# A graph layer and a mixture of experts on one core: the last stage's seven groups processed in five units

## The reference, cut to what matters

```
x = x + gnn(layernorm(x))        # gnn: [gat(W0) , gat(W1)] + input, then layer norm, * gamma + beta
x = x + ffn(layernorm(x))        # ffn: 8 experts, each node goes to its best 2

gat:   alpha over the edges into a node (softmax per head, 8 heads x 16 channels)
       out = segment_sum(xw[src] * alpha)
ffn:   logits = x @ Wg + bg;  top 2 -> softmax of the two logits
       out += w * (gelu(x @ W1[e] + b1[e]) @ W2[e] + b2[e])   for the 2 chosen experts
```

## Time and profile before

| | us |
|---|---|
| median of 3 runs (3034.85 to 3039.28) | 3036.93 |
| the profiled execution | 3038.06 |
| its span | 3036.2 |
| VectorE busy | 2092.3 (69%) |
| TensorE busy | 2122.6 (70%) |
| GpSimd busy | 1891.8 (62%) |
| ScalarE busy | 1786.1 (59%) |

### The profile page before, as it was taken

One profiled execution on the slowest core, in us unless ns is written; L12 is line 12 of the kernel. 1 busy time (PEld: TensorE's weight loads), 2 busy tenths in 40 slices (PEclk: granted clock), 3 DMA queues, 4 the chain that ended last, 5 costly groups with the idle time before them and its releaser, 6 DMA issues.

```text
span 3036.2 us, 42924 instructions
## 1 busy us (share of the span) xinstructions
PE 2122.6 (70%) x11674; PEld 2009.3 (66%) x11675; DVE 2092.3 (69%) x4422; ACT 1786.1 (59%) x2613; POOL 1891.8 (62%) x1868
## 2 busy tenths in 40 slices
PE   4600003778887888888878888603449999999998
PEld 2400003778887788787878787603438999999997
DVE  7678867777777777777777777788864444444443
ACT  5424424888888888888888888624433333333332
POOL 5777777777777777777777777777771222222222
PEclk8855556889998999898999898855559999999999
DMA  9446994444444444444444444555772222222222
GB/s 356 135 145 180 159 239 122 127 127 158 132 127 127 143 147 127 128 158 131 128 127 158 133 127 128 170 206 174 260 258 37 37 38 37 38 38 37 38 37 31
DMA packets 278910, 395.04 MB, mean 130 GB/s; under 512 B 156236, under 2 KB 231569, under 8 KB 272257
## 3 DMA queue, kind: packets, MB, share of 16 engines
q1 hardware_dynamic: 202945, 244.92, 25.8%
q0 software_dynamic: 74000, 145.58, 21.6%
q10 hardware_dynamic: 1840, 3.06, 0.3%
HBM read 201.61 MB, written 191.79 MB: 130 GB/s over the span
## 4 chain that ended last, share of the span: by engine, by line
POOL 47%; PE 25%; issue 16%; DVE 5%; DMA 2%; DVEq 1%; ACT 1%; SPq 1%; POOLq 0%; ACTq 0%
POOL AR L932 43%; PE ps L1440 12%; PE ps L1446 12%; POOL adstart L894 1%; POOL placed L999 1%; DMA tables<-AR 1%; POOL room L971 1%; DVE group_stats L1987 1%; ACT AR L1258 1%; DVE AR L1705 1%; SPq L379 0%; SPq L609 0%; DVE AR L2111 0%; DVE AR L2108 0%; DVE AR L2047 0%
## 5 line engine op out<-in xcount | busy, mean ns | idle before, releaser
L932 POOL DMA_INDIRECT AR<-tables,idx x1391 | 1329.8, 956 | 425.8 <-issue 423.5
L1354 PE MATMUL ps<-table_parts,onehot 128*128 128x408 f32 (+1 forms) x5848 | 1194.2, 369 | 304.5 <-ACT onehot L1214 213.3
L1354 PEld LDWEIGHTS ps<-table_parts,onehot 128*128 128x128 f32 x5848 | 1160.0, 208 | 338.7 <-DVE AR L1817 185.3
L1139 ACT COPY AR<-AR 128x1984 f32<-128x1984 f32 (+3 forms) x110 | 402.6, 3660 | 255.4 <-DVE AR L1752 212.6
L1008 POOL DMA_INDIRECT out<-AR,idb x105 | 185.0, 1762 | 567.6 <-issue 536.6
L1752 DVE TENSOR_TENSOR_SCAN AR<-ps,AR 128x512 f32<-128x512 f32 x404 | 454.2, 1197 | 0.0
L1440 PEld LDWEIGHTS ps<-AR 128*128 128x128 f32 x3360 | 393.2, 193 | 31.8 <-issue 26.5
L1440 PE MATMUL ps<-AR 128*128 128x128 f32 x3360 | 393.8, 276 | 26.4 <-DVE AR L2205 26.4
L1745 DVE TENSOR_TENSOR AR<-AR,ps 128x3968 f32<-128x3968 f32 (+1 forms) x51 | 357.5, 7010 | 5.8 <-ACT AR L1158 5.8
L1214 ACT ACTIVATE onehot<-onehot 128x2048 fp32r<-128x2048 f32 (+1 forms) x172 | 347.6, 2021 | 5.5
L2205 DVE COPY AR<-AR 128x1024 f32 x210 | 151.6, 722 | 207.2 <-PE ps L1440 205.7
(11 more groups left out here) (342 smaller groups left out, 2345.5 us busy)
## 6 DMA issues: line engine op xcount, KB each, us to landing
state<-AR SPq DMA_DIRECT2D x50, 2232.0 KB, 9.5
AR<-tables,idx POOLq DMA_INDIRECT x1440
AR<-in_L_ffn_W SPq DMA_DIRECT2D x16, 1024.0 KB, 9.7
AR<-placed SPq DMA_DIRECT2D x420, 32.0 KB
AR<-adstart SPq DMA_DIRECT2D x50, 248.0 KB, 4.0
adstart<-room SPq DMA_DIRECT2D x21, 496.0 KB, 13.5
tables<-AR SPq DMA_DIRECT2D x49, 136.0 KB
room<-tables SPq DMA_DIRECT2D x14, 476.0 KB, 4.4
```

The costliest lines, as they stand in the source:

```text
L932: pool.indirect_dma_start(out=G[s][:, j, 0:ROWT], out_offset=None, in_=table_rows, in_offset=bass.IndirectOffsetOnAxis(ap=idx[:, s, j:j + ...
L1139: return S.copy(to.rearrange("p j (h c) -> p j h c", h=HD)[:, :, :, a:z], of[:, :, 1:n + 1].rearrange("p (c h) j -> p j h c", h=HD)[:, :, ...
L1354: return T.matmul(bank[:, 0:z], mark, table_parts[:, k, v * w:v * w + z], start=(a == 0 and k == 0), stop=(a == LEV - 1 and k == PARTS - 1))
```

## The change

Groups are taken in units. `UNITS` for conv1 and all that follows is (0), (1), (2, 3), (4, 5), (6); `UNITS2` for conv2 is (0, 1), (2, 3), (4), (5, 6). The small instructions of a unit of two work on 14 tiles at once: `shares`, the weights (now a function of its own, `weights`), the scales, `choose`, `settle` and their waits. The per-tile instructions stay one for each tile, and `combine` (the products and sums of whole rows) and `conclude` stay one for each group. `ranks` of a pair has 16 products rather than 9. The buffers of the small values hold 14 tiles, the shares no longer two groups in turn.

The order changes on every engine:

- VectorE, unit u: `weights`, `combine` of its groups, statistics with the next unit's shares meanwhile, `choose(u - 1)`, `conclude` of its first group, `settle(u - 1)`, `conclude` of the second, second statistics (with conv2's last shares at u = 1, and its last pair behind them).
- ScalarE: the exponential of the next unit's shares stands ahead of the normalisation, that of the gate behind the first group's normalisation.
- GpSimd: conv2's group 6 is gathered ahead of conv1's 2, and conv1's 4 and 5 are gathered ahead of the first placement; group 6 of conv1 follows the placement of unit 0. A unit's placements go in one run.
- SyncE: `OWN_ORDER` takes conv2's 5 and 6 ahead of conv1's 2, and loads and stores follow the units.

The core of the diff:

```diff
+UNITS = ((0,), (1,), (2, 3), (4, 5), (6,))
+UNITS2 = ((0, 1), (2, 3), (4,), (5, 6))
+OWN_ORDER = ((1, 0), (1, 1), (1, 2), (1, 3), (1, 4), (0, 0), (0, 1), (1, 5), (1, 6), (0, 2), (0, 3), (0, 4), (0, 5), (0, 6))
...
             last_states2(5, 2, GRP)
-            for n in range(2, 4):
+            last_states2(6)
+            for n in range(2, 6):
                 last_states1(n)
-            last_states2(6)
...
-            for n in range(NG):
-                place(n)
-                if n + 4 < NG:
-                    last_states1(n + 4)
+            for u, unit in enumerate(UNITS):
+                pool.wait_ge(places_ready, u + 1)
+                for i, n in enumerate(unit):
+                    for k in range(2):
+                        for t in range(GRP):
...
+                if u == 0:
+                    last_states1(6)
...
+            for u, unit in enumerate(UNITS):
+                deviations(u, 0)
+                if u + 1 < NU:
+                    share_exps(0, u + 1)
+                act.wait_ge(group_scales_ready, 2 * u + 1)
+                for i, g in enumerate(unit):
+                    for t in range(GRP):
...
+                    if i == 0 and u >= 1:
+                        gate_exp(u - 1)
+                deviations(u, 1)
+                if u == 1:
+                    share_exps(1, 3)
+                act.wait_ge(group_scales_ready, 2 * u + 2)
+                for i, g in enumerate(unit):
+                    rows_normalised(g, i * GRP)
...
+            def ranks(u):
+
+                n = GRP * len(UNITS[u])
...
+                for d in range(1, n):
+                    T.matmul(ps[7][:, d * NEX:n * NEX], ones[:, :], mk[:, 0:(n - d) * NEX], start=False, stop=False)
...
+            def shares(k, u):
+
+                unit = (UNITS, UNITS2)[k][u]
...
+                for g in unit:
+                    dve.wait_ge((states1_gathered, states2_gathered)[k][g % 4], 16 * GRP * (g // 4 + 1))
...
             shares(1, 0)
             run_maxima(2)
-            shares(1, 1)
+            weights(1, 0)
             combine(1, 0)
             run_sums(2)
-            shares(1, 2)
-            fix_maxima(2)
             combine(1, 1)
+            fix_maxima(2)
             fix_sums(2)
-            shares(1, 3)
+            shares(1, 1)
+            weights(1, 1)
             combine(1, 2)
...
-            for g in range(NG):
-                combine(0, g)
+            for u, unit in enumerate(UNITS):
+                weights(0, u)
+                for g in unit:
+                    combine(0, g)
...
+                layer_stats([halves[g] for g in unit], u, 0, next_shares)
+                if u >= 1:
+                    choose(u - 1)
+                conclude(unit[0])
+                if u >= 1:
+                    settle(u - 1)
+                for g in unit[1:]:
+                    conclude(g)
...
+                layer_stats([X[:, g * GRP:(g + 1) * GRP, :] for g in unit], u, 1, last_shares2)
+                if u == 1:
+                    weights(1, 3)
+                    for g in UNITS2[3]:
+                        combine(1, g)
+            choose(NU - 1)
+            settle(NU - 1)
```

## The result

The changed kernel takes **3051.99 us** (median of 6 runs, 3051.11 to 3056.51), the kernel before 3038.04 us (median of the 6 runs beside them, 3034.85 to 3041.47). The ratio is **1.0048, 95% interval 1.0036 to 1.0061**: 14 us slower. 3056.0 was forecast, in a range of 3043 to 3064.

What follows compares the result with a forecast made beforehand. GpSimd's end, set by its placements or VectorE's chain to each `ipos`, was taken as the bound; stepping through waits, savings and tail put it at 2295.9 against 2276.77, 19.1 us later: 3056.0 us, range 3043 to 3064.

Steps and rivals of the forecast that it cites:

- Part 1: Conv2 in pairs and its new order: the fix-row wait is filled, VectorE's chain starts 4.4 us early, bounds 2 to 6.
- Part 2: Gathers' order on GpSimd: VectorE waits 13.5 us at `shares(0,2)` for group 3's gathers, between 9 and 17.
- rival 2: No wait at group 3, as GpSimd is not slowed or gathers land sooner: 10 us later than before, 3047; 7%.
- Part 3: Turned order within a unit: later normalisation (some 2.5 us in all), rank waits, and VectorE waits behind ScalarE's rows.
- rank waits: In `settle`, behind `conclude` of one group: a pair's ranks take 7.7 us, so VectorE waits 2.6 for each pair.
- the wait for the deviations of group 6: Behind pair (4,5), ScalarE does group 6's deviations after the pair's rows: VectorE waits 8.3 us.
- the logits: TensorE ends a pair 19.3 us after its scales: VectorE waits 1.4 us for the logits behind pair (4,5).
- Part 4: GpSimd's tail: 28 placements hang on `settle(3)` and 14 follow, 52.9 us against 37.4 before; a loss of 15.5 us.
- Rival 1: The clock rises while a pair is turned and ranked, VectorE's waits shrink by some 10 us: 3046; 8%.
- Rival 3: VectorE meets none of its new waits from `shares(0,2)` to `settle(3)`; GpSimd ends 7 us earlier, 3030; 9%.
- both losses: The gathers' order on GpSimd (wait of 13.5 us at `shares(0,2)`) and the 42-placement tail behind `settle(3)` (15.5 us).
- Rival 4: Paired work is bound by gaps, so pairs cost twice: about 5 us on top, 3061; 7%.

## Why the prediction was right, point by point

**What bounds the stage.** Right: GpSimd's end, as the later of its own placements and VectorE's chain to an `ipos`. Every line of the table above reads so.

**The start of VectorE's chain (Part 1).** Forecast 4.4 us early. `shares(0,0)` runs 42.6 us into the stage instead of 46.4, 3.8 early, inside the 2 to 6 (with the scatter of the start, 2.6 to 6.3 early in the runs above); the wait for the fix row is 1.24 instead of 4.30 us.

**The gathers (Part 2).** The mechanism and its place were right, the size was off: 9.12 us where 13.5 was summed, at the low end of 9 to 17. Two terms of the sum did most of it. The landing was put at 3.3 us by a gather of another stretch; here the last gather of group 3 ends at 2095.09 and VectorE runs at 2096.79, 1.7. And GpSimd was 2.2 us nearer: conv2's seven began 1.5 us earlier into the stage than I had them (54.9, not 56.4) and took 10.3 us, not 10.0; group 2's took 10.1 instead of 10.7, group 3's 8.4 instead of 8.75. VectorE came 0.5 later (76.3, not 75.7). The sooner landing was one of the two reasons that rival 2 gave; the wait itself did not go away, as it had it.

**The turned order (Part 3).** The rank waits came as 2.30 us, twice (forecast 2.6), the wait for the deviations of group 6 as 7.86 (8.3), the logits as 1.41 (1.4) and 0.33 (0.9). The exponentials were forecast to cost 0.5 to 1.0 us per unit, some 2.5 in all. In seven single units it was 0.4 to 0.6 for each of units 0 to 5. In after, undoing them gave nothing: unit 0's share lies ahead of a wait for a DMA, which takes up all that comes before it, and in the pairs the gain at the rows of unit 2 (0.3) is less than the new wait for the gate's exponential (0.49).

**The tail (Part 4).** 52.7 us for 42 placements forecast, 52.8 measured. That this tail is a loss of its own is shown by the run with only pair (4,5), which comes out as this reading had it, 292.2.

**The steps of the sum against the trace** (us into the stage; forecast, measured): unit (1) settled 146.1, 142.0; (2,3) 191.0, 185.9; (4,5) 235.8, 229.9; GpSimd done 288.7, 283.0. Of the 5.7 us between the last two, 3.7 were there when group 3's gathers were in (89.1, 85.4); the other 2 grew over the units behind, 0.4 to 1.0 us at a step. So the forecast of +19 and the measured +14 by the medians, +13.5 in the stage, differ in the main (3.7 of 5.6 us) by the landing and the pace of the gathers, and for the rest by what the units behind add, which I have not split up.

**Rival 1, the clock.** It did not rise. Around the turning of a pair's rows, the windows of after (columns as above):

```profile
2167.00:2190.00 23.00, 18.02 (x87) 17.61 (x86) 21.33 (x93) 16.75 (x35) 7.16 (x6) 0.50 0.40 141
```

TensorE is busy 18 of 23 us here, and stays at the lower level. The Trainium skill's rule on activity (TensorE: Matmul & The Clock Gate, What's actually happening), which spoke for this rival, showed nothing of itself in this stretch.

**Rival 3, the other side.** It asked for `settle(3)` before 2223.9, 216.7 into the stage; it came at 229.9 with both losses in and at 224.7 with the gathers in order. Of this last, 3.4 us were still a wait for the gathers; taken off, 221.3 is still too late for a pair (4,5). **Rival 4** (pairs cost double): `choose` of a pair took 4.8 us, less than the 5.1 of the sum.

**What the prediction lacked** shows in the experiments' expectations. It gave Part 2 and Part 4 as two losses, 9 to 17 and 15.5, and I expected each to come back whole when undone. Undoing the second gave about 2, because (2,3) binds right behind it with 70 placements; and undoing (2,3) gave nothing, because (4,5) does. The two bounds stood 2 us apart (GpSimd done at 277.9 and 275.8, both with the gathers in order), and only splitting both pairs brought the 13.5. What was not tried is a pair of other groups, (0,1) for instance, where GpSimd still has gathers to do.

## What to carry to other kernels

Work in pairs saves the producer's fixed costs, but it holds back the first half until the second is done; if a consumer that is nearly full takes the results, it stands idle for about one item and then has a backlog that nothing shortens. Before pairing, compute for each release "ready time plus all that the consumer has left from there", and pair only where this sum stays below the end as it is. The largest of these sums is the end, and the second largest says how little is won by mending the first. A saving that lies ahead of a wait for a DMA is worth nothing until that wait is gone. And where the start of a stage scatters, compare two runs from the last event ahead of the edit, not from the start.

## What the runs showed of the hardware

**GpSimd's indirect DMAs take longer while VectorE runs a large instruction with two operands in SBUF.** Of the 178 indirect DMAs of after's stage, 31 took over 1.2 us, up to 2.70, and every one of them overlaps a `tensor_tensor` of VectorE of 128x896 or 128x1792. Of the 124 that overlap none, not one took over 1.01. One place, VectorE against GpSimd:

```profile
2197.38 2.02 DVE L2167 TENSOR_TENSOR AR<-AR,gam 128x1792 f32<-128x1792 f32 x1
```

The placement that starts 0.18 us later, at 2197.56, took 2.67 us, the one at 2153.72, beside an instruction of the same line, 2.70; the one at 2293.41, with VectorE standing still, 0.96. The one at 2241.54, beside VectorE's `bn_stats` (one operand), took 0.96 as well. The Trainium skill, GPSIMD Engine Reference, section Key points, names a contention of the two engines for SBUF when VectorE has two SBUF inputs; the trace agrees. It is also why 70 placements took 95.0 us, 1.36 apiece, and the last 42 in after 1.26 apiece: in the run with (4) and (5) single, 8 of the 70 are such long ones, and in after none of the 42. A standing VectorE thus has a small return: GpSimd is quicker in its waits. That the second operand matters, and not the size alone, no run tried.

**The landing of a gather goes with how busy the DMA engines are.** From its instruction's end to the waiting instruction it was 1.7 us in after (DMA share 0.23 around it), 4.7 in the run with the gathers' old order (2085.36 to 2090.01, share 0.94), and 3.3 before (2197.80 to 2201.10, share 1.02 from 2197 to 2201). The gathers of after from 2007 to 2200 say the same: the 19 with a share under 0.5 between the end of the instruction and the landing took 1.5 to 1.6 us, the 15 with 0.9 and more 2.7 to 5.5. No run changes the load alone, so the share is what goes with it, not a cause that was tried.
